# Last key blocks of 384 and 256 in place of 512 and 128, and a stacked last half block in the gated FFNs' down projection

## What is computed

```python
# attention 1 (16 heads of 128, causal, 2048 rows of queries and keys)
q = rope(x @ Wq.T); k = rope(x @ Wk.T); v = x @ Wv.T
scores = einsum('bthd,bshd->bhts', q, k) * scale        # masked above the diagonal
y = einsum('bhts,bshd->bthd', softmax(scores), v)
return y / 3.0 @ Wo.T
# attention 0: one head of rank 32, same mask and softmax
# gated FFN (inner width 704)
g = einsum('th,ih->ti', xf, gate_w) * gate_s
u = einsum('th,ih->ti', xf, up_w) * up_s
hdn = silu(g) * u
out = einsum('ti,hi->th', hdn, down_w) * down_s
```

## Time and profile before

| | us |
|---|---|
| time before, median of 3 runs | 2054.95 (2053.97 to 2057.08) |
| profiled execution, its own time | 2052.96 |
| its span, first to last instruction | 2051.2 |
| PE busy | 1968.7 (96% of the span) |
| PE weight loads busy | 1782.8 (87%) |
| DVE busy | 1420.1 (69%) |
| ACT busy | 1316.8 (64%) |
| POOL busy | 964.7 (47%) |
| mean granted clock of PE | 0.995 |

### The profile page before, as it was taken

One profiled execution on the slowest core, in us unless ns is written; L12 is line 12 of the kernel. 1 busy time (PEld: TensorE's weight loads), 2 busy tenths in 40 slices (PEclk: granted clock), 3 DMA queues, 4 the chain that ended last, 5 costly groups with the idle time before them and its releaser, 6 DMA issues. The chain is left out here.

```text
span 2051.2 us, 40562 instructions
## 1 busy us (share of the span) xinstructions
PE 1968.7 (96%) x13863; PEld 1782.8 (87%) x13863; DVE 1420.1 (69%) x3580; ACT 1316.8 (64%) x3368; POOL 964.7 (47%) x986
## 2 busy tenths in 40 slices
PE   6988989998999999999999999999999999999899
PEld 4767867778899999999999999999999999998788
DVE  8348763644778777786877777787786878778553
ACT  4335623444768777777867777787777778677652
POOL 1642116634545536454553645545365454635252
PEclk9999999999999999999999999999999999999999
DMA  7752057700000000000000000000000000000010
GB/s 250 213 83 32 32 165 210 161 4 9 9 7 9 9 6 4 7 9 9 7 9 6 4 7 9 9 6 9 7 4 6 9 9 7 9 7 1 9 39 31
DMA packets 58283, 73.46 MB, mean 36 GB/s; under 512 B 9697, under 2 KB 44897, under 8 KB 57953
## 3 DMA queue, kind: packets, MB, share of 16 engines
q1 hardware_dynamic: 43488, 53.83, 8.1%
q0 software_dynamic: 14592, 17.04, 5.1%
HBM read 51.06 MB, written 19.80 MB: 35 GB/s over the span
## 5 line engine op out<-in xcount | busy, mean ns | idle before, releaser
L1141 ACT ACTIVATE phase_p<-phase_scores,phase_bias 128x512 f32<-128x512 f32 (+3 forms) x680 | 417.5, 628 | 114.8 <-DVE phase_bias L1129 113.3
L1186 DVE TENSOR_TENSOR phase_pt_lo<-phase_ring,phase_pt_hi 128x512 fp32r<-128x512 f32 (+3 forms) x680 | 390.6, 603 | 90.4 <-ACT phase_pt_hi L1181 87.1
L1181 ACT ACTIVATE phase_pt_hi<-phase_ring 128x512 fp32r<-128x512 f32 (+3 forms) x680 | 342.5, 536 | 110.9 <-PE phase_ring L1166 108.0
L1166 PE MATMUL phase_ring<-sb_ident,phase_p 128*128 128x128 f32 x2312 | 341.2, 274 | 10.5 <-ACT phase_p L1141 4.7
L132 PE MATMUL phase_y<-phase_pt_hi,phase_v_hi 128*128 128x256 f32 (+1 forms) x1152 | 342.8, 298 | 5.1 <-DVE phase_y_lo L2225 4.7
L133 PE MATMUL phase_y<-phase_pt_lo,phase_v_hi 128*128 128x256 f32 (+1 forms) x1152 | 323.9, 281 | 0.0
L134 PE MATMUL phase_y<-phase_pt_hi,phase_v_lo 128*128 128x256 f32 (+1 forms) x1152 | 323.6, 281 | 0.0
L1166 PEld LDWEIGHTS phase_ring<-sb_ident,phase_p 128*128 128x128 f32 x2312 | 270.9, 141 | 48.3 <-ACT phase_p L1141 12.7
L1122 DVE TENSOR_REDUCE phase_peaks<-phase_scores 128x1 f32<-128x512 f32 x408 | 272.4, 682 | 46.9 <-PE phase_scores L1109 44.5
L2248 POOL TENSOR_TENSOR phase_straight<-phase_rot,late_rope 64x512 f32<-64x512 f32 x128 | 164.3, 1283 | 274.2 <-ACT phase_rot L2120 274.2
L2265 POOL TENSOR_TENSOR sb_x<-sb_x,phase_part 128x512 f32<-128x512 f32 x128 | 165.7, 1294 | 254.4 <-ACT phase_part L2155 248.0
(11 more groups left out here) (269 smaller groups left out, 4889.8 us busy)
## 6 DMA issues: line engine op xcount, KB each, us to landing
phase_e_up<-expert_up SPq DMA_DIRECT2D x32, 352.0 KB, 5.0
phase_e_dn<-expert_down SPq DMA_DIRECT2D x32, 256.0 KB, 5.3
y_rows<-phase_zero SPq DMA_DIRECT2D x16, 512.0 KB, 7.8
sb_x<-y_rows POOLq DMA_DIRECT2D x16, 512.0 KB, 6.7
xn_rows<-phase_ln_xn SPq DMA_DIRECT2D x8, 512.0 KB, 3.0
late_raw_qk<-qk SPq DMA_DIRECT2D x16, 256.0 KB, 2.7
sb_x<-x SPq DMA_DIRECT2D x4, 512.0 KB, 5.7
phase_raw_up<-up SPq DMA_DIRECT2D x8, 256.0 KB, 5.0
```

Of the source, the lines that this page charges most:

```text
L1141: act.activation(self.p[:, at:at + width], self.scores[:, at:at + width], ACT.Exp, bias=self.bias[:, t % 2:t % 2 + 1], accum_out=self.sums ...
L1166: done = pe.transpose(bank[:, j * P:(j + 1) * P], self.p[:, (4 * place + j) * P:(4 * place + j + 1) * P], self.core.ident[:])
L1181: act.activation(hi, value, ACT.Copy).then_inc(*self.t_hi.one)
L1186: dve.tensor_tensor(lo, value, as_f32(hi), ALU.subtract).then_inc(*self.t_lo.one)
```

## The change

**Attention.** A new function `start(t, c)` gives the first key of a chunk. For the tiles 4, 8 and 12 the last chunk begins 128 keys earlier: the last two chunks become 384 and 256 wide, where they were 512 and 128. `blocks(t, b)` now gives the range of the key blocks, and scores, transposes, views and waits on older uses follow it. The number of chunks, their banks and the order of the steps stay. It concerns both attentions: 3 tiles in `Attention0`, 3 in each of the 16 heads of `Attention1`.

**Gated FFN.** The half block m = 5 no longer has zeros in the upper 64 partitions of `h_hi`. They get the low part of the same 64 rows (a new DVE step `dve_last_rest`, 64x512, once per chunk c, in place of POOL's), and the weights of those 64 rows are loaded into both halves of the partitions. Then `pe_down` needs two matmuls for this block in place of three: the stacked tile by the high and by the low weights. The load of the down weights becomes three DMAs (five blocks, then twice the 64 rows), and ACT waits for the third. POOL's zero fills go.

```diff
+    def start(self, t, c):
+        return CH * c - P if c and c == t // 4 and t % 4 == 0 else CH * c
+
     def width(self, t, c):
-        return (t % 4 + 1) * P if c == t // 4 else BANK
+        return (self.start(t, c + 1) if c < t // 4 else (t + 1) * P) - self.start(t, c)
...
     def blocks(self, t, b):
-        return min(4, t + 1 - 4 * b)
+        first = self.start(t, b) // P
+        return range(first, first + self.width(t, b) // P)
...
-                pe.wait_ge(*self.t_lo[0, t, j // 4])
+                pe.wait_ge(*self.t_lo[0, t, self.chunk(t, j)])
...
-        sp.dma_start(self.raw_dn[:], src["down1"]).then_inc(*self.down_in.one)
+        last = I1M - 1
+        sp.dma_start(self.raw_dn[:, 0:last, :], src["down1"][:, 0:last, :]).then_inc(*self.down_in.one)
+        for where in (slice(0, 64), slice(64, P)):
+            sp.dma_start(self.raw_dn[where, last, :], src["down1"][0:64, last, :]).then_inc(*self.down_in.one)
...
                 if j == 0:
-                    pe.wait_ge(*self.lo[tag, c, m])
-                done = products(pe, self.down_bank(j), [self.h_hi[:, c % 2, m, cols]], [self.h_lo[:, c % 2, m, cols]],
-                                [(self.dn_hi[:, m, :], self.dn_lo[:, m, :])], first=m == 0, last=m == I1M - 1)
-            done.then_inc(*self.down.one)
+                    pe.wait_ge(*self.lo((tag, c, m)))
+                if m < I1M - 1:
+                    products(pe, self.down_bank(j), [self.h_hi[:, c % 2, m, cols]], [self.h_lo[:, c % 2, m, cols]],
+                             [(self.dn_hi[:, m, :], self.dn_lo[:, m, :])], first=m == 0, last=False)
+            both = self.h_hi[:, c % 2, I1M - 1, cols]
+            pe.matmul(self.down_bank(j), both, self.dn_hi[:, I1M - 1, :], start=False, stop=False)
+            pe.matmul(self.down_bank(j), both, self.dn_lo[:, I1M - 1, :], start=False, stop=True).then_inc(*self.down.one)
...
-                    act.wait_ge(*self.down_in[tag])
+                    act.wait_ge(*self.down_in[tag, 2])
...
                 self.dve_piece(dve, c, m)
+                if c and m == 0:
+                    self.dve_last_rest(dve, c - 1)
...
                 self.dve_behind(dve, c, m)
+        self.dve_last_rest(dve, NCH - 1)
         self.dve_add(dve, NCH - 1, range(3))
...
+    def dve_last_rest(self, dve, c):
+        m = I1M - 1
+        dve.wait_ge(*self.hi[self.tag, c, m])
+        dve.tensor_tensor(self.h_hi[64:P, c % 2, m, :], self.mul[0:64, m % 2, :], as_f32(self.h_hi[0:64, c % 2, m, :]),
+                          ALU.subtract).then_inc(*self.lo_v.one)
...
-        pool.memset(as_f32(self.h_hi[64:P, :, I1M - 1, :]), 0.0).then_inc(*self.padded.one)
-        pool.memset(as_f32(self.h_lo[64:P, :, I1M - 1, :]), 0.0).then_inc(*self.padded.one)
-        pool.wait_ge(*self.padded[tag, 1])
```

54 lines of the change are left out of this document (30 added, 24 removed).

## The result

The changed kernel takes 2049.51 us (median of 9 runs, 2047.41 to 2053.93), the kernel before 2054.05 us beside it (9 runs, 2051.05 to 2057.13). The ratio is 0.9975, with a 95% interval of 0.9966 to 0.9984: 0.25% or 5.1 us faster, between 3.3 and 7.0. Forecast were 7.7 us and 2047.2 us. The direction and the range were right; the gain was a third smaller than forecast.

A forecast was written before the change was run, and what follows sets the result against it. PE's list of instructions was taken to bound the second attention, its successive matmuls the gated FFNs. 3.2 + 0.15 + 3.84 + 0.6 + 0.4 - 0.5 = 7.7 us off 2054.95 gives 2047.2 us, range 2044.5 to 2050.8.

The forecast's parts named there:

- Scores: Tiles 4, 8 and 12: a pair of chunks costs 0.875 us, was 0.97; 48 pairs in the second attention, 4.8 us.
- Rival C: Matmuls cost by columns alone, so the new attention split gains nothing; 4.35 us in all, 2050.6; chance 0.03.
- VectorE and ScalarE in the attention: Exponentials and peaks cost the same in sum; the unknown peak of 384 columns taken as 551 ns, bounds 423 and 682.
- What of it reaches the end: Second attention: tiles 8 and 12 keep 32 x 0.10 = 3.2 us of the 4.8, tile 4 keeps 0.
- rival A: Tile 4 keeps its gain too, as the chains behind it move up; 9.3 us in all, 2045.6; chance 0.11.
- Down projection: Both gated FFNs: one matmul fewer per tile, 16 tiles x 2 FFNs x 0.12 = 3.84 us, all on PE's path.
- Low part of the half block: VectorE's step replaces GpSimd's: 0.6 and 0.4 us won ending the first FFN; hidden by 0.2 in the second.
- Loads and fills: Down weights landing later cost 0.4 us in the first FFN (at most 1.0), 0.1 in the second (at most 0.6).
- The sign that I had named for it: ScalarE's wait for the down weights stays 2.6 and 1.7 us long; longer if the loads land later than allowed.
- Rival D: The down weights land later than allowed, 1.9 us per FFN; 4.4 us gained in all, 2050.5; chance 0.06.
- E: The three down-weight DMAs go one behind the other, some 5 us per FFN; slower, 2057.2 us; chance 0.03.
- Sum: All terms of attention, down projection, half block and loads together: 7.7 us faster, 2047.2 us.

The follow-up runs named there:

- experiments 6 and 7: The changed kernel with the new chunk widths for tile 4 alone (6) or tile 8 alone (7); one run each, 2052.03 and 2052.27 us.
- experiments 3 and 9: The changed kernel, its second accumulating DMA later: behind two restored zero fills (3), or waiting for the second rounded up block (9); 2049.32 and 2048.51 us.
- experiments 10 and 11: The changed kernel, ScalarE rounding down weights one piece later (10), and also the accumulating DMA waiting for the second up block (11); 2045.50 and 2046.81 us.
- experiment 1: The kernel before with the new chunk widths alone, both gated FFNs as before; 2052.27 us against 2054.98, ratio 0.9986.

## Why the forecast was right, and where it was off

**Scores.** Right. In a full stream the triple of 384 columns and the one of 256 take 0.53 and 0.36 us; tile 8 of the changed kernel (compare):

```profile
982.71 0.34 PE L1115 MATMUL phase_scores<-phase_k_hi,phase_q_hi 128*128 128x384 f32 x1
...
983.24 0.28 PE L1115 MATMUL phase_scores<-phase_k_hi,phase_q_hi 128*128 128x256 f32 x1
...
983.60 0.60 PE L1173 MATMUL phase_ring<-sb_ident,phase_p 128*128 128x128 f32 x4
```

983.60 - 982.71 = 0.89 against 0.97. Over all 48 such pairs of chunks the mean from the first start to the next instruction's fell from 1.019 to 0.924 us, 0.095 less. Rival C is out. The 128-column matmuls of before come 0.112 us apart in these means, the 256-column ones 0.118. The Trainium skill's page "TensorE: Matmul & The Clock Gate", section "LDWEIGHTS (loading the stationary operand)", gives P / 1.2 ns for P columns, an estimate of 107 ns for 128, and the spacing of 0.112 us is near that. By the isolated gap of its section "Back-to-back issue gap" nothing would have been won, and 0.095 us per pair was.

**VectorE and ScalarE in the attention.** Right, and the unknown value was the one taken. Groups by line and shape of the changed kernel (ScalarE's within the second attention; compare):

```profile
L1147 ACT ACTIVATE phase_p<-phase_scores,phase_bias 128x384 f32<-128x384 f32 x112 | 66.3, 592 | 22.7 <-DVE phase_bias L1135 21.5
L1147 ACT ACTIVATE phase_p<-phase_scores,phase_bias 128x256 f32<-128x256 f32 x112 | 53.8, 481 | 0.0
```

```profile
L1126 DVE CUSTOM_DVE_ANT_0 phase_scores<-phase_scores,sb_hide 128x256 f32<-128x256 f32 x119 | 50.4, 424 | 1.0
...
L1128 DVE TENSOR_REDUCE phase_peaks<-phase_scores 128x1 f32<-128x384 f32 x51 | 27.9, 547 | 0.0
...
L1790 DVE TENSOR_TENSOR phase_h_hi<-phase_act,phase_h_hi 64x512 fp32r<-64x512 f32 x8 | 5.5, 685 | 0.9 <-ACT phase_h_hi L1727 0.7
```

The peak of 384 columns takes 547 ns (551 estimated).

**What of it reaches the end.** The step that failed in part. Tile 4: right (0), and rival A is out. Tiles 8 and 12: I took all of 3.2 us; the changed kernel's profile keeps 0.30 us per pair of heads, 8 x 0.30 = 2.4 us, and the mean of the profiles 0.25, 2.0 us. From the first score to the last the seven profiles with the split and the changed FFNs take 1412.28 to 1413.68 us, mean 1413.04, the three without it 1414.71 to 1415.24, mean 1414.99: 1.95 us, and the profiled pair of the table at the top is the luckiest. The failed sentence is "I see no wait of PE behind them that hangs on work begun before them": behind tile 12 the next scores wait for an exponential whose start is set by VectorE's queue, and it had 0.24 us of slack, for a saving of 0.13. Two steps behind the transposes in the even heads give back as much. I had looked for waits that exist, not for ones that lay 0.1 to 0.2 us off.

**Down projection.** Right. Each of the first three blocks takes 8.03 us from its first matmul to its last, 8.51 before: 0.48 us, 4 x 0.12, and the 17 matmuls of a tile take 2.04 us.

**Low part of the half block.** Its step takes 685 ns (689 taken). At the end of the first FFN (PE, compare):

```profile
490.10 0.39 PE L1650 MATMUL phase_down_ps<-phase_dn_hi,phase_h_hi 128*128 128x256 f32 x1 [0.25 <-DVE phase_h_hi L1790]
...
494.92 1.06 PE L285 MATMUL phase_turn_ps<-sb_ident,phase_ln_xn 128*128 128x128 f32 x8 [0.25 <-ACT phase_ln_xn L278]
```

The first wait fell from 0.94 to 0.25, the second from 0.43 to 0.25: 0.87 us, 1.0 predicted. In the second FFN it was to be hidden by 0.2 us; it isn't quite (VectorE, then PE):

```profile
2037.40 0.68 DVE L1790 TENSOR_TENSOR phase_h_hi<-phase_act,phase_h_hi 64x512 fp32r<-64x512 f32 x1
```

```profile
2037.96 0.28 PE L134 MATMUL phase_down_ps<-phase_dn_hi,phase_h_lo 128*128 128x256 f32 x1
2038.13 0.38 PE L1650 MATMUL phase_down_ps<-phase_dn_hi,phase_h_hi 128*128 128x256 f32 x1
2038.36 0.28 PE L1651 MATMUL phase_down_ps<-phase_dn_lo,phase_h_hi 128*128 128x256 f32 x1
```

It ends at 2038.08, and the steps to 2038.13 and 2038.36 are 0.17 and 0.23 in place of 0.12 each: 0.16 us. I had counted when PE asks, 1.8 us, and the step's end, 1.6, but not that an answer so close costs too.

**Loads and fills.** The term that was mis-sized most. For the first FFN I allowed 0.4 us and at most 1.0 for later landing. The rounding of the down weights moved by 1.55 us in the profiled pair, and by 1.1 in the mean of the profiles (17.84 against 16.33 and 17.24), while PE started 1.0 us sooner and got nothing from it. The first down matmul moved by 1.54 us in the pair and, against the mean of the two with old FFNs, by 1.4 (34.77 against 33.3), of which 0.4 is the low clock of experiments 6 and 7. The prediction put the blame first on three issues in place of one, and the 2 us that the accumulating DMA moves up inside the same 1.0; experiments 3 and 9 show that the DMA is the cause. The sign that I had named for it, a longer wait of ScalarE for the down weights, didn't come: that wait fell from 2.62 to 2.08 us, because ScalarE reached it later, held up by the up weights. Rival D has the right mechanism and over half its 1.9 us in the first FFN. In the second, where there is no such DMA, nothing was lost: the last of the three loads lands 6.57 us behind the first one's issue in the mean, one load 6.25, but the first down matmul comes 23.36 to 23.81 us behind the first `pe_up` with the changed FFNs (experiments 10 and 11 apart), and 23.47 and 24.09 with the old ones. E is out (its price left 0.5 us of the loads in twice: 2056.8, not 2057.2). The fills' effect on VectorE was missed altogether.

**Sum.** The second attention 2.0 in place of 3.2; the second FFN's down blocks 1.8 in place of 1.92; the first FFN, from first load to last down matmul, 121.26 in the mean of the five profiles with its form, 122.6 in the mean of the two with the old one: 1.4 where 1.92 + 1.0 - 0.4 = 2.5 was predicted. Both means hold low-clock stretches of about 1 us each, five in the five profiles and one in the two; my estimate without them is 120.25 against 122.0, so 1.7. 2.0 + 1.8 + 1.7 and the 0.15 of the first attention, not measured by itself, make 5.7 us, within the 3.3 to 7.0 of the runs. It is close to the case that the prediction puts at the end of its range, half of the attention's gain and the loads at their worst: 5.0 us. That the median shows 5.1 is no finer confirmation than that.

Open: experiment 1 gained only 0.9 us over the 14 heads in its profile (1241.38 against 1242.33 and 1242.24), half of what the same attention gained beside the changed FFNs. One profile can't tell chance from cause.

## What to carry to other kernels

Work that is taken away ahead of a DMA issue moves the DMA up: look at what will then be in flight, and put a wait in its place if the engines are full. A saving on the bounding engine is safe only up to the slack of the next semaphore, so read for each saving not the waits that exist but the nearest release that came just in time. And a wait of another engine is worth removing only when the bounding engine waits with it; the same edit was worth nothing before the change, and 1.6 to 2.4 us at the first down matmul behind it.

## What the runs showed of the hardware

- VectorE's two normalising steps of 128x256 take 0.73 us, and 2.27 us while GpSimd fills memory. In each of the four profiles with fills PE's first up matmul comes 1.0 us later; in experiments 3 and 9 the first down matmul doesn't move with it.
- A wait that is released just as PE arrives costs PE about 0.11 to 0.16 us, though hardly any of it is listed as idle: 0.05 ahead of the waiting matmul and 0.06 to 0.11 as a longer step behind it. The weight load then starts 0.03 us or less ahead of its matmul, where it started 0.12 us ahead without the wait.
- With an accumulating DMA of 512 KB issued 2 us sooner the fourth block of up weights (256 KB) was rounded at 11.55 to 13.03 us in place of 10.58 to 11.24, 1.4 us later in the mean, and the down weights that came behind it 1.1 us later.
- Stretches of low granted clock inside a stage (0.60 to 0.82 over 5 us) come and go between profiles of the same code, at three places of the first FFN, and cost about 1.0 us each time.
